# Splitting half of the u weights of a Mamba block into one-pass products

## The chip, the cores and the metric

One Trainium2 chip, one core of it. The metric is the device time of one execution in microseconds, the median of several runs. The kernel computes a whole two-layer perceiver block with x in (2, 64, 1024), so 128 token rows fill the 128 partitions. Engines: TensorE (PE; PEld is its weight load), VectorE (DVE), ScalarE (ACT), GpSimd (POOL), and SyncE (SP), which issues the DMAs.

## The reference, cut to what matters

Six sublayers follow each other, each adding to x. The change lies in the second one, a Mamba block, of which this is the part that matters:

```python
proj = hidden_states @ W_in.T                     # (128, 1024) @ (1024, 4096)
u, gate = jnp.split(proj, 2, axis=-1)             # 2048 columns each
x = conv_general_dilated(u ...)                   # depthwise, 4 taps in time
u = jax.nn.silu(x + conv_b)
ssm_p = u @ Wx.T                                  # 96 columns: dt, B, C
...                                               # softplus, scan over 64 steps of 16 states
y = (ys + u * D_param) * jax.nn.silu(gate)
return y @ W_out.T
```

All data is float32.

## The kernel before

Every engine has its own instruction stream, written out by hand, with semaphores between them. Weights come as units of 1 MB: 128 partitions x (4 k tiles x 512 columns), into a ring of seven slots; SyncE issues them in the order of `unit_list`, each when the last use of its slot is over (`last_use`, `uses`, L533). w_in has 16 units. A group j of 512 output columns takes two of them: k tiles 0 to 3 from unit 2j, 4 to 7 from unit 2j+1. Groups 0 to 3 (NG = 4) are u, groups 4 to 7 the gate. The small tables of the Mamba block (`mamba_in`, L520 to L524) are queued ahead of unit w_in 4.

The left side is h, the normalized x, transposed to `hT` (k tiles 0 to 3 copied by ScalarE at L686, 4 to 7 by VectorE at L1478). `w_in_product(j, k)` (L1003, matmul at L1012) multiplies in full float32 into a PSUM bank; the profile records each such matmul as two. After the last k tile it raises `proj_psum`.

What follows for a u group, engine by engine:

- ScalarE `proj_copy(j)` (L693) copies the group out of PSUM. TensorE transposes it, `turn(j)` (L931), two k tiles into the next group. 
- VectorE `conv_in(j)` (L1484) copies the transpose to `uT`. ScalarE `last_tap(j)` (L736) multiplies the newest tap, VectorE `conv(j)` (L1501) adds three taps; for the last group VectorE does the newest tap too (L1495).
- ScalarE `half_tanh(j)` (L701), then VectorE `silu(j)` (L1516).

Their orders are: ScalarE: proj_copy(j), last_tap(j), half_tanh(j-1) for j = 0 to 2, then proj_copy(3), half_tanh(2), half_tanh(3). VectorE: conv_in(0), conv(0), conv_in(1), silu(0), conv(1), conv_in(2), silu(1), conv(2), conv_in(3), silu(2), conv(3), silu(3). TensorE: the four u groups with turns 0 to 2 in them, one gate product, turn(3), five gate products, `small_projection` 0 to 2 (L1029), one gate product, `small_projection(3)`, and then the time steps and the scan. `small_projection(3)` needs silu(3); everything behind it hangs on it.

From w_out on the kernel already uses split products: ScalarE `high(m)` (L795) copies a unit, rounded to float32r, VectorE `low(m)` (L1621) subtracts that from the unit, and TensorE multiplies high by high, high by low (both at L965) and low by high (L972), one pass each, from `unit_halves`. The left side is split in the same way into `split` (L683, L1474). The memory `rounded` (the same as `plain`) is not in use while w_in is multiplied.

Of the kernel before, what the change touches and what calls it, by code (L numbers as in the profile page):

```python
# [12 lines left out]
ALU = mybir.AluOpType  # L13
ACT = mybir.ActivationFunctionType
AX = mybir.AxisListType.X
F32 = mybir.dt.float32
# [8 lines left out]
KT = D // P  # L25
UK = 4
UN = 512
UNIT = UK * UN
# [13 lines left out]
NG = DT // GD  # L42
# [46 lines left out]
def perceiver(nc, dram, out):  # L89
    units = unit_list()  # L90
    first = {}
# [5 lines left out]
    with ExitStack() as stack:  # L97
# [3 lines left out]
        def sem(name):  # L101
            return stack.enter_context(nc.semaphore(name))
# [4 lines left out]
        hT = sb("hT", [P, KT, P])  # L107
# [10 lines left out]
        split = sb("split", [P, 2, KT, P], F32R)  # L118
        psum = stack.enter_context(nc.psum_tensor("psum", [P, 8, 512], F32))

        def carve(tile, start, *dims):
            size = 1
            for d in dims:
                size *= d
            ap = tile[:, start:start + size]
            if len(dims) == 2:
                ap = ap.rearrange("p (a b) -> p a b", a=dims[0])
            if len(dims) == 3:
                ap = ap.rearrange("p (a b c) -> p a b c", a=dims[0], b=dims[1])
            return ap  # L130
# [78 lines left out]
            rounded[:, 2 * UNIT:4 * UNIT], rounded[:, 0:2 * UNIT], arena_r[:, 11392:11392 + 2 * UNIT])]  # L209


        w_ar = carve(arena, 0, KT, NE * RANK + NE)
        lora_b = carve(arena, 1088, D)
        bk = carve(arena, 19040, D)
# [66 lines left out]
        hT_hi = sem("hT_hi")  # L281
# [15 lines left out]
        q1T_ready = sem("q1T_ready")  # L297
        q_done = sem("q_done")

        edge_zero = sem("edge_zero")  # L300
        conv_halved = sem("conv_halved")
        first_tap = sem("first_tap")
        proj_psum = sem("proj_psum")
# [113 lines left out]
        def uses(*signals, split=False):  # L417
            nonlocal middle
            for signal in signals:
                if signal is None:  # L420
                    middle += 1
                    signal = (unit_used, middle)
                if split:
                    split_units.append(len(last_use))
                    split_done.append(signal)
                    signal = (unit_low, len(split_done))
                last_use.append(signal)

        for j in range(NB):
            uses(None, (proj_psum, j + 1))  # L430
        uses(None, None)
        uses(None, None)
        for nh in range(2):
# [36 lines left out]
        def slot(n):  # L470
            return place(n).rearrange("p (k n) -> p k n", k=UK)

        def arrived(eng, n):
            if n in spare:

                eng.wait_ge(unit_in[SLOTS + 1], 16 * SPARE)
            else:
                eng.wait_ge(unit_in[slot_of[n]], 16 * slot_of[:n + 1].count(slot_of[n]))
# [5 lines left out]
        def proj_bank(j):  # L484

            return j % 3 if j <= NG else 4

        def turn_bank(j):

            return 3 + j % 2 if j < NG else 5  # L490
# [158 lines left out]
        def _(act):  # L649
# [34 lines left out]

            act.wait_ge(hT_psum, 1)
            act.activation(hT[:, 0:4, :], psum[:, 6, :], ACT.Copy).then_inc(hT_lo, 1)  # L686

            def proj_copy(j):

                act.wait_ge(proj_psum, j + 1)  # L690
                if j >= 3:
                    act.wait_ge(projT_psum, j - 2)
                act.activation(proj[:, j % 3, :], psum[:, proj_bank(j), :], ACT.Copy).then_inc(proj_sb, 1)  # L693
# [38 lines left out]
            def last_tap(g):  # L732

                act.wait_ge(projT_read, g + 1)
                for k in range(GD * g, GD * g + GD):
                    last = act.activation(uc[:, k, :].rearrange("p (b t) -> p b t", b=B), uT[:, k, :, CK - 1:], ACT.Identity,  # L736
                                          bias=conv_b[:, k:k + 1], scale=conv_w[:, k, CK - 1:CK])
                last.then_inc(first_tap, 1)

            for j in range(3):  # L740
                proj_copy(j)
                last_tap(j)
                if j:
                    half_tanh(j - 1)
# [136 lines left out]
            for r in range(GQ):  # L881
                last = act.activation(krep[:, :, r, :], krot.rearrange("p (g d) -> p g d", g=HKV), ACT.Copy)
# [43 lines left out]
        def _(pe):  # L926
# [13 lines left out]
            for nh in range(2):  # L940
                for kh in range(2):
                    for b in range(B):
# [3 lines left out]
                        for k in range(UK):  # L946
# [6 lines left out]
                            last = pe.matmul(psum[rows, 2 + nh, :], ones64, right, **at)  # L953
# [47 lines left out]
            w_in = first["w_in"]  # L1001

            def w_in_product(j, k):  # L1003

                u = 2 * j + k // UK
                if k == 0 and j >= 3:
                    pe.wait_ge(*((proj_sb, j - 2) if j <= NG else (proj_sb, j) if j > NG + 1 else (projT_read, NG)))
                if k % UK == 0:
                    pe.wait_ge(hT_lo, 1)
                    pe.wait_ge(hT_hi, 1)  # L1010
                    arrived(pe, w_in + u)
                last = pe.matmul(psum[:, proj_bank(j), :], hT[:, k, :], slot(w_in + u)[:, k % UK, :], start=(k == 0),  # L1012
                                 stop=(k == KT - 1))
                if k % UK == UK - 1:
                    last.then_inc(proj_psum if k == KT - 1 else unit_used, 1)
# [3 lines left out]
            def gate_products(count):  # L1019

                for _ in range(count):
                    w_in_product(*next(gate_tiles))
# [48 lines left out]
            def scan_input(s):  # L1071
# [17 lines left out]
                                     stop=True)  # L1089
                last.then_inc(dbu_ready, 1)  # L1090

            for j in range(NG):
                for k in range(KT):
                    if j and k == 2:
                        turn(j - 1)
                    w_in_product(j, k)
            gate_products(1)
            turn(3)
            gate_products(5)
# [89 lines left out]
            for k in range(KT):  # L1189
                last = pe.matmul(psum[:, 2, 0:NE * RANK + NE], hT[:, k, :], w_ar[:, k, :], start=(k == 0), stop=(k == KT - 1))  # L1190
# [148 lines left out]
            for nh in range(2):  # L1339
                for part, signal in enumerate((hs_high, hs_low)):  # L1340
                    for k in range(KT):
                        if nh == 0 and k % 4 == 0:
                            pe.wait_ge(signal, 9 + k // 4)
                        last = pe.matmul(psum[:, 4 + nh, :], split[:, part, k, :], onehot[:, k, UN * nh:UN * nh + UN],  # L1344
                                         start=(part == 0 and k == 0), stop=(part == 1 and k == KT - 1))
# [8 lines left out]
            for a in range(MH // 2):  # L1354
                pe.wait_ge(g_hi if a >= 4 else g_lo, 1)
                for m in range(2):
                    for r in range(2):
                        rows = slice(MD * r, MD * r + MD)
                        at = 256 * (a % 2) + P * m
                        last = pe.matmul(psum[:, 4 * r + a // 2, at:at + P], up[rows, a, P * m:P * m + P], gT[rows, a, :],  # L1360
                                         start=True, stop=True)
# [22 lines left out]
        def _(dve):  # L1384
# [91 lines left out]

            dve.wait_ge(hT_psum, 2)
            dve.tensor_copy(hT[:, 4:8, :], psum[:, 7, :]).then_inc(hT_hi, 1)  # L1478
            dve.wait_ge(mamba_in, 80)
            dve.wait_ge(edge_zero, 2)  # L1480

            def conv_in(g):
                dve.wait_ge(projT_psum, g + 1)
                dve.tensor_copy(uT[:, GD * g:GD * g + GD, :, CK - 1:],  # L1484
                                psum[:, turn_bank(g), :].rearrange("p (k b t) -> p k b t", k=GD, b=B)).then_inc(projT_read, 1)

            def conv(g):


                dve.wait_ge(projT_read, g + 1)  # L1490
                if g < NG - 1:
                    dve.wait_ge(first_tap, g + 1)
                else:
                    for k in range(GD * g, GD * g + GD):
                        last = dve.tensor_scalar(uc[:, k, :].rearrange("p (b t) -> p b t", b=B), uT[:, k, :, CK - 1:],  # L1495
                                                 conv_w[:, k, CK - 1:CK], conv_b[:, k:k + 1], ALU.mult, ALU.add)
                    step(last)
                for j in range(CK - 1):
                    for k in range(GD * g, GD * g + GD):
                        to = uc[:, k, :].rearrange("p (b t) -> p b t", b=B)  # L1500
                        last = dve.scalar_tensor_tensor(out=to, in0=uT[:, k, :, j:j + L], scalar=conv_w[:, k, j:j + 1], in1=to,  # L1501
                                                        op0=ALU.mult, op1=ALU.add)
                    if j < CK - 2:
                        step(last)
                last.then_inc(conv_half, 1)

            def silu(n):

                dve.wait_ge(tanh_ready, n + 1)
                if n < NG:  # L1510
                    to = uc[:, GD * n:GD * n + GD, :].rearrange("p k t -> p (k t)")
                    of = to
                else:
                    to = sg[:, GD * (n - NG):GD * (n - NG) + GD, :].rearrange("p k t -> p (k t)")
                    of = psum[:, turn_bank(n), :]
                dve.scalar_tensor_tensor(out=to, in0=tanh[:, n % 2, :], scalar=1.0, in1=of, op0=ALU.add,  # L1516
                                         op1=ALU.mult).then_inc(gated, 1)
# [2 lines left out]
            dve.tensor_scalar(small[:, 320:416], small[:, 320:416], 0.5, None, ALU.mult).then_inc(conv_halved, 1)  # L1520
            dve.wait_ge(conv_halved, 1)
            conv_in(0)
            conv(0)
            conv_in(1)
            silu(0)
            conv(1)
            conv_in(2)
            silu(1)
# [373 lines left out]
```

## Time and profile before

| what | value |
|---|---|
| median of 3 runs | 400.17 us (397.13 to 401.21) |
| profiled execution | 399.9 us, its span 398.1 us |
| mean granted TensorE clock | 0.949 |
| TensorE busy (PE) | 351.0 us, 88% of the span |
| VectorE, ScalarE, GpSimd busy | 269.5, 198.3, 115.4 us |
| DMA, whole span | 81.33 MB, mean 204 GB/s |
| L1012 (w_in products), 128 records | 63.6 us |

The profile is of one execution. Busy time says how long an engine worked, not whether anybody waited for it. The chain that ended last is followed back from the last instruction, at each step to what released it. In a timeline the brackets give the idle time ahead of an instruction and what ended it. PEclk is the granted TensorE clock as a share of full speed: 1.00 is 2.4 GHz, 0.50 is 1.2 GHz. Matmuls are pipelined, so the duration of a single record overlaps the next; distances between starts say what one costs.

### The profile page before, as it was taken

Reading aid. Unit: us, or ns where it says so; the run is one execution under the profiler, and the core shown is the slowest. Engines: PE = TensorE matmul, PEld = TensorE weight load, DVE = VectorE, ACT = ScalarE, POOL = GpSimd, SP = SyncE. Lnnn points to the kernel's source line nnn. Section 1 sums busy time; section 2 is a strip of 40 time slices with the busy share of each in tenths; the row PEclk is TensorE's granted clock in tenths of the full one; section 3 lists DMA queues with packets and bytes.
Section 4 is the critical chain, followed back from the end, with each engine's and each line's share of the span. In section 5 each row is a group of like instructions: output and inputs, shape, how many; then the busy total and the mean of one; then the engine's idle time right before and its main releaser. Section 6 shows DMA issues by size and latency. Waiting matters only on the chain.

```text
span 398.1 us, 4954 instructions
## 1 busy us (share of the span) xinstructions
PE 351.0 (88%) x1894; PEld 222.8 (56%) x1894; DVE 269.5 (68%) x334; ACT 198.3 (50%) x397; POOL 115.4 (29%) x97
## 2 busy tenths in 40 slices
PE   0784999999999989999899897899979698697996
PEld 0432444553556656556566585787323476585885
DVE  2756046947887999998971887685721798765282
ACT  2970034169999687677621554363021476430160
POOL 3500000023999888889900000002000000400000
PEclk9997799999999999999999989699999899669899
DMA  6999987744003020253138798298999991000001
GB/s 260 421 423 376 391 342 266 272 133 185 2 0 107 2 81 26 105 198 126 53 115 331 268 421 340 68 358 327 413 423 370 428 420 62 2 2 0 2 2 53
DMA packets 12824, 81.33 MB, mean 204 GB/s; under 512 B 2094, under 2 KB 2350, under 8 KB 3519
## 3 DMA queue, kind: packets, MB, share of 16 engines
q1 hardware_dynamic: 11614, 78.23, 50.6%
q10 hardware_dynamic: 1154, 2.70, 2.0%
q8 instruction: 15, 0.25, 0.2%
q14 instruction: 9, 0.07, 0.1%
q0 software_dynamic: 32, 0.07, 0.0%
HBM read 80.34 MB, written 0.52 MB: 203 GB/s over the span
## 4 chain that ended last, share of the span: by engine, by line
PE 57%; DVE 15%; POOL 10%; issue 7%; DMA 6%; ACT 3%; POOLq 0%; SPq 0%; DVEq 0%; ACTq 0%
PE psum L1012 10%; PE psum L965 9%; PE psum L1132 6%; PE psum L1235 6%; DMA ring<-in_ctx 6%; PE psum L1088 5%; POOL arena L618 5%; PE psum L931 4%; PE psum L972 4%; PE psum L1156 3%; PE psum L1344 2%; DVE arena L1578 2%; POOL arena L621 2%; PE psum L1379 2%; POOL plain L618 2%
## 5 line engine op out<-in xcount | busy, mean ns | idle before, releaser
L768 ACT ACTIVATE arena<-arena 128x126 f32<-128x126 f32 x256 | 76.5, 389 | 9.7 <-DVE arena L1578 9.3
L1012 PE MATMUL psum<-ring,hT 128*128 128x512 f32 x128 | 63.6, 627 | 0.8 <-issue 0.8
L1578 DVE TENSOR_TENSOR_SCAN arena<-arena,psum 128x1024 f32<-128x1024 f32 x24 | 54.2, 2272 | 3.2 <-PE psum L1088 3.0
L618 POOL TENSOR_TENSOR arena<-arena 128x1024 f32<-128x1024 f32 x20 | 47.2, 2360 | 5.4 <-DVE arena L1578 5.4
L1621 DVE TENSOR_TENSOR rounded<-ring,rounded 128x2048 fp32r<-128x2048 f32 x16 | 36.5, 2285 | 10.4 <-ACT rounded L795 10.4
L1132 PEld LDWEIGHTS psum<-arena,ident 128*128 128x128 f32 x292 | 35.6, 192 | 13.8 <-issue 10.0
L795 ACT ACTIVATE rounded<-ring 128x2048 fp32r<-128x2048 f32 x16 | 30.6, 1912 | 21.9 <-PE psum L972 14.0
L558 POOL TENSOR_TENSOR small<-small 128x1 f32<-128x1 f32 x6 | 3.3, 554 | 127.0 <-DVE small L1402 127.0
L1012 PEld LDWEIGHTS psum<-ring,hT 128*128 128x128 f32 x128 | 23.3, 199 | 29.1 <-issue 29.1
L1132 PE MATMUL psum<-arena,ident 128*128 128x128 f32 x292 | 37.3, 278 | 1.6 <-POOL arena L621 1.6
L1088 PE MATMUL psum<-plain 64*128 64x512 f32 x128 | 36.1, 641 | 1.7 <-DVE arena L1578 1.4
L931 PE MATMUL psum<-ident,h 128*128 128x128 f32 x48 | 10.9, 402 | 27.6 <-DVE h L1405 16.0
L965 PE MATMUL psum<-rounded,split 128*128 128x512 f32 x96 | 27.7, 436 | 0.3 <-DVE rounded L1621 0.3
L931 PE MATMUL psum<-ident,arena 128*128 128x128 f32 x120 | 21.2, 306 | 7.3 <-ACT arena L901 2.6
L931 PEld LDWEIGHTS psum<-ident,h 128*128 128x128 f32 x48 | 8.5, 204 | 31.1 <-DVE h L1405 19.4
L931 PEld LDWEIGHTS psum<-ident,arena 128*128 128x128 f32 x120 | 14.9, 153 | 19.0 <-issue 6.9
L1235 PE MATMUL psum<-ring,arena 128*64 128x512 f32 x96 | 24.4, 593 | 0.0
L965 PEld LDWEIGHTS psum<-rounded,split 128*128 128x128 f32 x96 | 20.1, 215 | 5.6 <-ACT split L683 0.6
L683 ACT ACTIVATE split<-psum 128x512 fp32r<-128x512 f32 x10 | 6.0, 598 | 31.2 <-PE psum L931 31.1
L621 POOL TENSOR_TENSOR arena<-arena 128x256 f32<-128x256 f32 x23 | 21.0, 917 | 1.6
L1578 DVE TENSOR_TENSOR_SCAN plain<-arena,psum 128x1024 f32<-128x1024 f32 x8 | 18.2, 2272 | 4.1 <-PE psum L1088 4.1
L675 ACT ACTIVATE arena<-ring,small 128x2048 uint8<-128x2048 f32 (+1 forms) x9 | 16.9, 1900 | 8.0 <-DMA ring<-in_ctx 8.0
(207 smaller groups left out, 579.4 us busy)
## 6 DMA issues: line engine op xcount, KB each, us to landing
ring<-in_w_in SPq DMA_DIRECT2D x16, 1024.0 KB, 7.5
ring<-in_ctx SPq DMA_DIRECT2D x13, 1024.0 KB, 10.0
ring<-in_w_out SPq DMA_DIRECT2D x8, 1024.0 KB, 4.8
ring<-in_ctx_t SPq DMA_DIRECT2D x7, 1024.0 KB, 5.1
ring<-in_w_base SPq DMA_DIRECT2D x4, 1024.0 KB, 4.8
ring<-in_x_wk SPq DMA_DIRECT2D x4, 1024.0 KB, 7.7
ring<-in_a_wo SPq DMA_DIRECT2D x4, 1024.0 KB, 9.4
ring<-in_x_wq SPq DMA_DIRECT2D x3, 1024.0 KB, 8.9
```

Of the source, the lines that this page charges most:

```text
L618: pool.tensor_tensor(state[s % STATES], state[s % STATES], c, ALU.mult).then_inc(prod_ready, 1)
L621: pool.tensor_tensor(v[:, :, L * 4:L * 6], v[:, :, L * 4:L * 6], v[:, :, L * 6:L * 8], ALU.add).then_inc(pairs_ready, 1)
L768: last = act.activation(to, of, ACT.Exp, scale=a_par[:, k, state_no:state_no + 1])
L795: act.activation(unit_halves[m % 3][:, 0, :, :], slot(split_units[m]), ACT.Copy).then_inc(unit_high, 1)
L931: last = pe.transpose(psum[:, bank, P * k:P * k + P], tile[:, c:c + P], ident[:, :])
L965: pe.matmul(psum[:, bank, :], left(0, k0 + k), unit[:, w, k, :], start=(start and k == 0 and w == 0), stop=False)
L1012: last = pe.matmul(psum[:, proj_bank(j), :], hT[:, k, :], slot(w_in + u)[:, k % UK, :], start=(k == 0), stop=(k == KT - 1))
L1088: last = pe.matmul(psum[:, input_bank(s, b), :], du[rows_of(b), left], bdiag[rows_of(b), right, :], start=True, stop=True)
L1132: last = pe.matmul(psum[:, 6 + g % 2, cols], ident[:, :], v[:, n, :, :], start=(s % 2 == 0 and n == 0), stop=(s % 2 == 1 and n == count - 1))
L1235: last = pe.matmul(psum[L * b:L * b + L, bank, :], left[:, UK * kh + k, L * b:L * b + L], slot(u0 + b)[:, k, :], start=(kh == 0 and k == 0 ...
L1578: dve.tensor_tensor_scan(state[s % STATES], dA[:, s % 3, :], psum[:, p:p + 2, :].rearrange("p a b -> p (a b)"), 0.0, ALU.mult, ALU.add).th ...
L1621: dve.tensor_tensor(unit[:, 1, :, :], slot(split_units[m]), unit[:, 0, :, :].bitcast(F32), ALU.subtract).then_inc(unit_low, 1)
```

## The change

For the four u groups, the second unit (k tiles 4 to 7) no longer goes through `w_in_product` but through split products. ScalarE gets one copy of the upper half of hT into `split`, and four copies u_high(j) of a weight unit, j = 0 and 1 ahead of proj_copy(0), 2 and 3 between proj_copy(j-2) and last_tap(j-2). VectorE gets the matching subtractions: u_low(0) and u_low(1) ahead of conv_in(0), u_low(2) between conv_in(0) and conv(0), u_low(3) between silu(0) and conv(1). The halves alternate between two buffers in `rounded`. A split unit's ring slot comes free at its u_low. TensorE issues 12 one-pass products in place of four full ones.

```diff
+        u_halves = [rounded[:, 2 * UNIT * n:2 * UNIT * n + 2 * UNIT].rearrange("p (a k n) -> p a k n", a=2, k=UK)
+                    for n in range(2)]
...
         for j in range(NB):
-            uses(None, (proj_psum, j + 1))
+            uses(None, (u_unit_low, j + 1) if j < NG else (proj_psum, j + 1))
...
             act.activation(hT[:, 0:4, :], psum[:, 6, :], ACT.Copy).then_inc(hT_lo, 1)
+            act.wait_ge(hT_hi, 1)
+            act.activation(split[:, 0, 4:8, :], hT[:, 4:8, :], ACT.Copy).then_inc(u_left_high, 1)
+
+            def u_high(j):
+
+                n = first["w_in"] + 2 * j + 1
+                arrived(act, n)
+                if j >= 2:
+                    act.wait_ge(proj_psum, j - 1)
+                act.activation(u_halves[j % 2][:, 0, :, :], slot(n), ACT.Copy).then_inc(u_unit_high, 1)
+
+            u_high(0)
+            u_high(1)
...
             for j in range(3):
                 proj_copy(j)
+                if j < 2:
+                    u_high(2 + j)
                 last_tap(j)
...
+            def u_split_products(j):
+
+                pe.wait_ge(u_left_low, 1)
+                pe.wait_ge(u_unit_low, j + 1)
+                unit = u_halves[j % 2]
+                for k in range(UK):
+                    for w in range(2):
+                        pe.matmul(psum[:, proj_bank(j), :], split[:, 0, UK + k, :], unit[:, w, k, :], start=False, stop=False)
+                for k in range(UK):
+                    last = pe.matmul(psum[:, proj_bank(j), :], split[:, 1, UK + k, :], unit[:, 0, k, :], start=False,
+                                     stop=(k == UK - 1))
+                last.then_inc(proj_psum, 1)
+
             for j in range(NG):
-                for k in range(KT):
+                for k in range(UK):
                     if j and k == 2:
                         turn(j - 1)
                     w_in_product(j, k)
+                u_split_products(j)
...
             dve.tensor_copy(hT[:, 4:8, :], psum[:, 7, :]).then_inc(hT_hi, 1)
+            dve.wait_ge(u_left_high, 1)
+            dve.tensor_tensor(split[:, 1, 4:8, :], hT[:, 4:8, :], split[:, 0, 4:8, :].bitcast(F32),
+                              ALU.subtract).then_inc(u_left_low, 1)
+
+            def u_low(j):
+
+                dve.wait_ge(u_unit_high, j + 1)
+                unit = u_halves[j % 2]
+                dve.tensor_tensor(unit[:, 1, :, :], slot(first["w_in"] + 2 * j + 1), unit[:, 0, :, :].bitcast(F32),
+                                  ALU.subtract).then_inc(u_unit_low, 1)
+
+            u_low(0)
+            u_low(1)
...
             conv_in(0)
+            u_low(2)
             conv(0)
             conv_in(1)
             silu(0)
+            u_low(3)
             conv(1)
```

## Rows read from the trace of the kernel before

**Rows 1.** The chain that ended last, 43 to 83 us: start, duration, what.

```profile
50.72 6.87 PE psum L1012 x16
...
65.37 0.70 DVE arena L1484
...
79.77 1.13 PE psum L1029 x8
```

**Rows 2.** Timeline of VectorE, 36 to 75 us: start, duration, work, idle time before.

```profile
37.76 0.69 DVE L1478 COPY hT<-psum 128x512 f32<-128x512 f32 x1 [1.60 <-PE psum L931]
...
50.83 0.69 DVE L1484 COPY arena<-psum 128x512 f32<-128x512 f32 x1 [8.71 <-PE psum L931]
53.30 3.49 DVE L1501 SCALAR_TENSOR_TENSOR arena<-arena,small 128x128 f32<-128x128 f32 x12 [1.79 <-ACT arena L736]
58.06 0.69 DVE L1484 COPY arena<-psum 128x512 f32<-128x512 f32 x1 [1.27 <-PE psum L931]
60.99 0.69 DVE L1516 SCALAR_TENSOR_TENSOR arena<-arena 128x512 f32<-128x512 f32 x1 [2.23 <-ACT arena L701]
61.60 3.48 DVE L1501 SCALAR_TENSOR_TENSOR arena<-arena,small 128x128 f32<-128x128 f32 x12
65.37 0.69 DVE L1484 COPY arena<-psum 128x512 f32<-128x512 f32 x1 [0.28 <-PE psum L931]
...
72.30 0.68 DVE L1484 COPY arena<-psum 128x512 f32<-128x512 f32 x1
```

**Rows 3.** Timeline of ScalarE, 36 to 60 us, same columns.

```profile
48.60 0.60 ACT L693 ACTIVATE arena<-psum 128x512 f32<-128x512 f32 x1 [11.10 <-PE psum L1012]
51.55 1.65 ACT L736 ACTIVATE arena<-arena,small 128x128 f32<-128x128 f32 x4 [2.35 <-DVE arena L1484]
55.91 0.60 ACT L693 ACTIVATE arena<-psum 128x512 f32<-128x512 f32 x1 [2.71 <-PE psum L1012]
```

**Rows 4.** The chain, 200 to 262 us: f32 products followed by one-pass products.

```profile
203.99 10.30 PE psum L1156 x24
214.29 1.86 PE psum L965 x8
216.15 0.92 PE psum L972 x4
```

**Rows 5.** Source lines of the split in later stages: duration ns min/median/max, starts.

```profile
L795 ACT ACTIVATE rounded<-ring x16: 1897/1913/1923, 192.1 to 357.2; 128x2048 fp32r<-128x2048 f32 x16
...
L1621 DVE TENSOR_TENSOR rounded<-ring,rounded x16: 2275/2283/2293, 199.3 to 359.2; 128x2048 fp32r<-128x2048 f32 x16
```

**Rows 6.** Busy times by window: span, PE, PEld, DVE, ACT, POOL, PEclk, DMA, GB/s.

```profile
44.00:45.00 1.00, 1.00 (x4) 0.36 (x3) 0.00 (x0) 0.00 (x0) 0.00 (x0) 0.79 1.02 418
```

**Rows 7.** The page: GB/s moved in each of 40 slices of the span.

```profile
GB/s 260 421 423 376 391 342 266 272 133 185 2 0 107 2 81 26 105 198 126 53 115 331 268 421 340 68 358 327 413 423 370 428 420 62 2 2 0 2 2 53
```

**Rows 8.** Timeline of TensorE: small projections, and two bursts that follow idle time.

```profile
75.96 2.81 PE L1029 MATMUL psum<-arena 128*128 128x96 f32 x24
...
250.08 1.97 PE L931 MATMUL psum<-ident,h 128*128 128x128 f32 x8 [3.15 <-DVE h L1405]
...
294.58 1.33 PE L931 MATMUL psum<-ident,arena 128*128 128x128 f32 x8 [2.31 <-ACT arena L867]
```

**Rows 9.** The chain behind the idle stretch that ends at 250.08 us.

```profile
252.05 3.61 PE psum L965 x8
255.66 1.15 PE psum L972 x4
256.81 1.83 PE psum L965 x8
258.65 0.91 PE psum L972 x4
```

**Rows 10.** Busy times by window after the same two idle stretches.

```profile
250.00:252.00 2.00, 1.92 (x9) 1.69 (x9) 0.62 (x3) 0.60 (x1) 0.00 (x0) 0.50 0.00 0
294.00:295.00 1.00, 0.42 (x4) 0.42 (x4) 0.00 (x0) 1.00 (x4) 0.00 (x0) 1.00 0.99 418
```

More of the change, by code:

```diff
@@ L298, in perceiver @@
         q_done = sem("q_done")
+        u_left_high = sem("u_left_high")
+        u_left_low = sem("u_left_low")
+        u_unit_high = sem("u_unit_high")
+        u_unit_low = sem("u_unit_low")
         edge_zero = sem("edge_zero")
```

## The prediction, made before the kernel ran

> **What bounds the kernel now.** I read the page first, where TensorE has by far the most busy time, which does not yet say that it ends the waits. The change touches only the stage that projects w_in and convolves (about 36 to 80 us), so next I read the chain of work that ended last in that stage, then the timelines of VectorE and ScalarE in it, and last, from later stages, the price of the same operations where the kernel already uses them.
>
> In the chain the reader is to see a change of hands. Up to 65.3 us it runs on TensorE alone: 16 records of 0.43 us (6.87 us) and then the transposes of `turn`, and it delivers a group of columns each 7.31 us (copies at 48.60 and 55.91) [rows 1, 3]. From 65.37 us it runs on VectorE and ScalarE (copy, last tap, half tanh, silu, taps) until 79.7 us, and TensorE takes over with `small_projection(3)` at 79.77 us [rows 1]. The VectorE timeline shows how close that was even before [rows 2]. A loop of conv_in, last_tap (ScalarE, 1.65 us), tanh, silu and three taps takes 58.06 to 65.08 us (61.60 + 3.48) = 7.02 us, against the 7.31 us in which TensorE delivers; VectorE was ready 0.28 us before the third group [rows 2, 3]. The third loop, where nothing is waited for from TensorE, takes 65.37 to 72.30 = 6.93 us [rows 2]. So a faster TensorE is worth little here, and added VectorE time is worth its full price wherever it lands in this loop outside an existing wait.
>
> **The change part by part.** *TensorE.* In each of four u groups the last four k tiles leave as full-precision products (8 records of 0.429 = 3.43 us by 6.87/16) and come back as 12 one-pass products. Later stages price these: 24 f32 records take 10.30 us (0.429 each), and directly behind them 8 one-pass products take 1.86 and 4 take 0.92, thus 2.78 us for 12, with no gap at the switch [rows 4]. A later dozen takes 1.83 + 0.91 = 2.74 [rows 9]. I take 2.73. Saved: 3.43 - 2.73 = 0.70 us a group, 2.8 us in four. The Trainium skill (FP8 and Floating Point Precision, TensorE Precision Notes) counts a true FP32 product as four passes; by that count three passes of four would save a quarter of 3.43, or 0.86 us a group. The trace's one-pass product (1.86/8 = 0.23 us) is slightly dearer than half an f32 record (0.21), and the sum goes by the trace.
>
> *First split, ahead of group 0.* hT's upper half is there at 37.76 + 0.69 = 38.45 us [rows 2]. ScalarE then rounds it (0.60, as its other copies of 128x512 [rows 3]), then u_high(0) and u_high(1), 1.91 us each [rows 5]: done at 39.1, 41.0 and 43.0. VectorE: left low 0.69 (as its copy), u_low(0) from 41.0 to 43.3, u_low(1) to 45.6, 2.28 us each [rows 5]. TensorE spends until about 44.8 on the first unit, because the granted clock is at its lower level (1.2 GHz) until about 44.4 and at 2.4 GHz after (0.79 of full speed in the microsecond from 44) [rows 6]. So u_low(0) is 1.5 us early, and all of this lies in idle time: ScalarE sat idle 11.1 us before 48.60, VectorE 8.7 before 50.83 [rows 2, 3]. Cost 0; if the clock rose as soon as 40 us, TensorE would wait some 0.6 us.
>
> *Arrivals.* The bytes queued up to unit w_in 3 are 13.1 MB (x 0.5, eight ctx and four w_in units of 1.05), up to w_in 5 with the 1.6 MB of tables ahead of w_in 4 16.8 MB, up to w_in 7 18.9 MB. By the GB/s row 14.7 MB had moved by 39.8 us and 18.6 by 49.8 (slices of 9.95 us) [rows 7]. So they land near 36, 45 and 51 us, and the ScalarE reads them at 41.0, 48.5 and 55.1: no wait. The slots of the split units come free at u_low instead of at the group's end, but only loads of gate units (first used after 67 us) follow from it: 0.
>
> *ScalarE in the loop.* u_high(2) and u_high(3) stand between proj_copy(j) and last_tap(j). ScalarE sat idle 2.35 us there in group 0, waiting for VectorE's conv_in [rows 3]. With 1.91 us it is free 0.4 us before conv_in ends. Behind it are queued last_tap, half_tanh and the next proj_copy; none is delayed. Cost 0.
>
> *VectorE in the loop.* With T0 (start of the copy out of PSUM) = 48.60 - 0.70 = 47.90, and 7.31 - 0.70 = 6.61 a group, T1 = 54.51, T2 = 61.12, T3 = 67.73. conv_in comes 2.15 to 2.23 us behind T [rows 2, 3].
> Group 0: conv_in 50.13, u_low(2) 50.83 to 53.11 (the old wait for last_tap, 1.79 us, covers most of it), conv(0) to 56.61. conv_in(1) is due at 54.51 + 2.15 = 56.66: hidden by 0.05 us.
> Group 1: u_low(3) stands behind silu(0) and ahead of conv(1), where VectorE never waited: full price. conv_in(2) at 56.66 + 6.93 + 2.28 = 65.87 (was 65.37), although TensorE has the group ready at 63.3.
> Group 2: conv_in(3) at 65.87 + 6.93 = 72.80 (was 72.30). From here every step is as before: silu(3) and small_projection(3) are 0.5 us later.
>
> *What TensorE does with its time.* proj_copy(3) is queued behind last_tap(2) and half_tanh(1) on ScalarE and now starts near 68.8 instead of at T3, so turn(3) waits some 0.9 us until 69.4. Ahead of small_projection(3) TensorE then has ten f32 records (4.3), the first three small projections (2.81) [rows 8] and two f32 records (0.86), so that it stands idle from about 77.9 to 80.3. The 2.8 us gained end there. Behind it comes the same chain, all moved by +0.5 us; no load later is issued by a clock of its own.
>
> **Sum.** -2.8 us of TensorE work, of which 0 reaches the end; the loop gains 1.8 from the earlier start of group 1 (72.30 - (56.66 + 2 x 6.93)) and pays 2.28: +0.5 us. The profiled execution took 399.9 us, so 400.4; the median of the runs is 400.17, 0.3 above it, and against that the forecast is 400.7 us. About 1% (4 us) is what a measurement of this kernel can tell from no change.
>
> **Rivals.**
> *Faster: u_low costs nothing on the path.* If the third split fits into waits (a tap loop shorter than I read, or TensorE still the one that ends the stage), the loop ends at 56.66 + 2 x 6.93 = 70.5, 1.8 us earlier: 398.4; with TensorE in charge to the end all 2.8: 397.4. For it: 2.2 us of VectorE idle in each group [rows 2]. Against: that idle lies ahead of silu, and u_low(3) stands behind it. It decides if u_low(3) runs ahead of silu(0). 12%.
>
> *Slower: the new idle stretches lower TensorE's clock.* Two gaps (0.9 and 2.4 us) appear where TensorE had none. A gap of 2.31 us ahead of 294.58 left the clock at 1.00; behind one of 3.15 us ahead of 250.08 it was 0.50 [rows 8, 10]. There the 8 transposes took 1.97 us against 1.33 at 294.58, the next 8 products 3.61 against 1.86 and 4 more 1.15 against 0.92: +2.6 us [rows 4, 8, 9]. If that falls on the work behind 80 us: 0.5 + 2.6 = +3.1, 403.8. The gap I expect is nearer the harmless one, and mostly small products lie ahead of it: 10%. The Trainium skill (TensorE: Matmul & The Clock Gate, What's actually happening) says that the throttled level is the default and activity lifts it, which speaks against a change that opens gaps; the trace has an outcome of each kind.
>
> *The one-pass products save nothing* (their loads of weights not hidden, or TensorE waiting for u_low(0)): T1 stays 55.91, conv_in(1) 58.06, then 58.06 + 2 x 6.93 + 2.28 = 74.20: +1.9 us, 402.1. Against it are the 12 such products at 0.23 us directly behind f32 ones [rows 4]. 8%.
>
> **How the numbers follow.** Forecast 70% (400.7, own range 399.5 to 402), rivals 12, 10 and 8%. The range for 8 in 10 reaches from the first (398.4) to nearly the second (403.8), widened below for the spread of single runs: 398.2 to 403.6. None but a fallen clock with a second mishap passes +1%, none alone reaches -1%. Faster by over 1%: 4%; within: 88%; slower: 8%.
>
> **What would show it.** In the profile after: L1012-type f32 records fall from 128 to 96 and 48 one-pass products appear in the stage; the copies out of PSUM come 6.6 us apart, then the fourth late; conv_in(1) near 56.7, conv_in(2) near 65.9, conv_in(3) near 72.8, small_projection(3) near 80.3; a TensorE gap of 2 us or more ahead of it with PEclk 1.00. The forecast is wrong if the last two come earlier than 79.8, if the clock is at 0.50 past 70 us, or if the difference comes from beyond 95 us, where I expect only the shift.

## The result, and the profile after

| | kernel before | changed kernel |
|---|---|---|
| median of 20 runs | 399.88 us (396.98 to 401.40) | 401.12 us (400.15 to 402.88) |
| ratio | 1 | 1.0040, 95% interval 1.0021 to 1.0059 |
| profiled execution (its span) | 399.9 us (398.1) | 402.87 us (401.1) |
| granted clock in it, mean | 0.949 | 0.940 |

The change made the kernel slower by 1.6 us (0.8 to 2.4) by the ratio, which goes by all runs; the two medians are 1.2 us apart. Either is within 1% of before. The forecast was +0.5 us, 400.7.

The page of the changed kernel shows what was bought and what was paid. In the fence are its TensorE, VectorE and ScalarE totals and the clock row. TensorE's own busy time did not fall, though 2.8 us of work are gone.

```profile
PE 351.7 (88%) x1910; PEld 227.2 (57%) x1910; DVE 278.8 (70%) x339; ACT 205.8 (51%) x402; POOL 115.4 (29%) x97
...
PEclk9996799989999999999999989899989899569899
```

VectorE and ScalarE have 9.3 and 7.5 us more. In the clock row the slice from 80 us is an 8, where before had a 9.

The next fence is the timeline of VectorE in the changed kernel (start, duration, work, idle time before). It answers to [rows 2].

```profile
50.03 0.69 DVE L1533 COPY arena<-psum 128x512 f32<-128x512 f32 x1 [4.43 <-PE psum L953]
50.64 2.28 DVE L1523 TENSOR_TENSOR rounded<-ring,rounded 128x2048 fp32r<-128x2048 f32 x1
52.84 3.48 DVE L1550 SCALAR_TENSOR_TENSOR arena<-arena,small 128x128 f32<-128x128 f32 x12
56.59 0.69 DVE L1533 COPY arena<-psum 128x512 f32<-128x512 f32 x1 [0.27 <-PE psum L953]
59.52 0.69 DVE L1565 SCALAR_TENSOR_TENSOR arena<-arena 128x512 f32<-128x512 f32 x1 [2.24 <-ACT arena L721]
60.13 2.28 DVE L1523 TENSOR_TENSOR rounded<-ring,rounded 128x2048 fp32r<-128x2048 f32 x1
62.33 3.48 DVE L1550 SCALAR_TENSOR_TENSOR arena<-arena,small 128x128 f32<-128x128 f32 x12
65.73 0.69 DVE L1533 COPY arena<-psum 128x512 f32<-128x512 f32 x1
...
72.66 0.68 DVE L1533 COPY arena<-psum 128x512 f32<-128x512 f32 x1
```

L1533 is conv_in, L1523 u_low, L1550 the taps, L1565 silu. u_low(2) at 50.64 fills a wait. u_low(3) at 60.13 does not: VectorE has just been idle for 2.24 us, waiting for the tanh, and then pays 2.28 us. conv_in(2) and (3) come at 65.73 and 72.66, against 65.37 and 72.30 before.

On TensorE the time saved turns up as idle time, ahead of turn(3) and of small_projection(3):

```profile
67.49 1.02 PE L1034 MATMUL psum<-ring,hT 128*128 128x512 f32 x2
69.15 0.66 PE L953 MATMUL psum<-ident,arena 128*128 128x128 f32 x4 [0.64 <-ACT arena L713]
...
76.59 1.05 PE L1034 MATMUL psum<-ring,hT 128*128 128x512 f32 x2
80.12 1.13 PE L1051 MATMUL psum<-arena 128*128 128x96 f32 x8 [2.48 <-DVE arena L1565]
```

small_projection(3) starts at 80.12, 0.35 us later than before (79.77). So far the forecast holds. But at 81.7 us, 1.6 us behind the end of the idle stretch, the granted clock falls to its lower level, 1.2 GHz, and stays there until 85.1. The fence is the busy times by window of the changed kernel (columns as in [rows 6]; the figure before the last two is PEclk).

```profile
78.00:80.00 2.00, 0.00 (x0) 0.00 (x0) 1.30 (x4) 0.63 (x1) 0.00 (x0) 1.00 0.00 0
80.00:82.00 2.00, 1.88 (x10) 1.38 (x11) 0.71 (x6) 0.00 (x0) 0.00 (x0) 0.93 0.00 0
82.00:84.00 2.00, 2.00 (x4) 0.73 (x3) 0.95 (x10) 0.60 (x1) 0.86 (x1) 0.50 0.35 49
84.00:86.00 2.00, 2.00 (x6) 0.76 (x4) 1.34 (x2) 0.28 (x2) 0.55 (x1) 0.72 0.85 352
86.00:88.00 2.00, 2.00 (x17) 1.83 (x16) 0.00 (x0) 1.82 (x2) 1.35 (x1) 1.00 0.31 127
```

It falls on the three gate products that lead the chain there. These six records took 2.60 us before, now 4.30 (the chain that ended last, changed kernel):

```profile
80.12 1.13 PE psum L1051 x8
81.25 4.30 PE psum L1034 x6
85.55 0.11 PE psum L1070
...
95.43 2.30 DVE plain L1629
```

The first scan step starts at 95.43. From VectorE's copy of the small projection (81.29) that is 14.14 us; before it was 93.60 - 80.94 = 12.66. So 0.35 us came from the loop and 1.48 from the clock: 1.83 us at the start of the scan. The profiled pair ends 3.0 us apart; the other 1.2 us come late, where the clock falls at many places in both kernels. In this pair it also fell at 296.7 us in the changed kernel, and not in before: behind 94 us the clock was low for 34.2 us in all, against 31.4.

### The profile page after: what moved, and what is told of

Read it like the earlier page. It is cut to its first block, busy times and chain, and to the rows that moved or that the text cites. A ratio compares the mean times of both kernels' runs of the same rounds, so it can differ in the third digit from the quotient of the medians.

```text
span 401.1 us, 4998 instructions
## 1 busy us (share of the span) xinstructions
PE 351.7 (88%) x1910; PEld 227.2 (57%) x1910; DVE 278.8 (70%) x339; ACT 205.8 (51%) x402; POOL 115.4 (29%) x97
## 4 chain that ended last, share of the span: by engine, by line
PE 56%; DVE 15%; POOL 10%; issue 7%; DMA 6%; ACT 4%; POOLq 0%; SPq 0%; DVEq 0%; ACTq 0%
PE psum L987 10%; PE psum L1034 7%; PE psum L1271 7%; PE psum L1168 6%; DMA ring<-in_ctx 6%; PE psum L1110 5%; POOL arena L625 5%; PE psum L994 4%; PE psum L953 4%; PE psum L1192 3%; DVE arena L1550 3%; PE psum L1380 2%; DVE arena L1629 2%; POOL arena L628 2%; PE psum L1415 2%
## 5 line engine op out<-in xcount | busy, mean ns | idle before, releaser
L1034 PE MATMUL psum<-ring,hT 128*128 128x512 f32 x96 | 52.0, 657 | 0.8 <-issue 0.8
L953 PE MATMUL psum<-ident,h 128*128 128x128 f32 x48 | 9.4, 360 | 27.7 <-DVE h L1441 16.0
L987 PE MATMUL psum<-rounded,split 128*128 128x512 f32 x96 | 28.9, 452 | 0.8 <-ACT split L690 0.5
L1034 PEld LDWEIGHTS psum<-ring,hT 128*128 128x128 f32 x96 | 17.6, 206 | 20.9 <-issue 20.6
L953 PEld LDWEIGHTS psum<-ident,h 128*128 128x128 f32 x48 | 7.2, 182 | 31.2 <-DVE h L1441 19.4
```

The source lines that it names most:

```text
L953: last = pe.transpose(psum[:, bank, P * k:P * k + P], tile[:, c:c + P], ident[:, :])
L987: pe.matmul(psum[:, bank, :], left(0, k0 + k), unit[:, w, k, :], start=(start and k == 0 and w == 0), stop=False)
```

## The experiments

The theories were these. **L**: the loss is u_low(3), at its full price in the loop of VectorE and ScalarE (the steps from one conv_in to the next). **C**: the idle stretch that the change opens on TensorE makes the clock fall, and the work behind it pays. **T**, named for the first run: later stages lose, whatever the u stage does. The ratio is to before on the same chip and goes by all runs, so it need not be that of the two medians. Four numbers are read from every trace: the start of small_projection(3), the idle stretch ahead of it, the clock behind it, and the way from VectorE's copy of the small projection to the first scan step.

| kernel | median, us | ratio (95%) | idle stretch | clock behind it | way to the scan |
|---|---|---|---|---|---|
| before | 399.88 | 1 | 0.1 | 1.00 | 12.66 |
| changed | 401.12 | 1.0040 (1.0021 to 1.0059) | 2.48 | 0.50 | 14.14 |
| f1_low_first | 398.13 | 0.9940 (0.9917 to 0.9962) | 1.11 | 1.00 | 12.66 |
| f2_pad_gap | 401.23 | 1.0020 (1.0000 to 1.0041) | 0.77 | 1.00 | 12.65 |
| f3_before_delay | 401.27 | 1.0020 (1.0004 to 1.0037) | 1.94 | 1.00 | 12.66 |
| f4_three_groups | 398.52 | 0.9942 (0.9922 to 0.9963) | 0.41 | 1.00 | 12.66 |
| g1_after_again | 402.37 | 1.0069 (1.0041 to 1.0097) | 2.49 | 0.50 | 13.94 |
| g2_pad_again | 401.96 | 1.0043 (1.0011 to 1.0075) | 0.77 | 1.00 | 12.65 |
| g3_low_first_and_tile | 397.47 | 0.9951 (0.9924 to 0.9979) | 0.25 | 1.00 | 11.79 |
| g4_longer_gap | 404.63 | 1.0118 (1.0088 to 1.0148) | 3.90 | 0.50 | 14.56 |

The median of before was 400.32 us beside the f kernels and 399.69 beside the g kernels.

### f1_low_first: the third subtraction ahead of silu

```diff
             conv_in(1)
-            silu(0)
             u_low(3)
+            silu(0)
             conv(1)
```

> The changed kernel with one swap on VectorE: u_low(3) runs ahead of silu(0) instead of behind it. Theory L (the loss is u_low(3) at full price in the loop of VectorE and ScalarE): VectorE sat idle 2.24 us ahead of silu(0), u_low(3) lasts 2.28, so the loop gets back 2.2 us; conv_in(3) near 70.5 us, small_projection(3) near 77.9, TensorE arrives there at 77.6 without a gap, the clock stays at 1.00 behind it, and the median is 1.5 to 2 us below the kernel before (398 to 398.5). Theory C (the loss is the clock that falls behind the gap, in some executions): also gone here, since the gap goes. Theory T (later stages lose, whatever the u stage does): the median stays 1 to 1.5 us above before although small_projection(3) is early.

Measured: 398.13 us, 0.6% below before. The VectorE timeline of this kernel shows u_low(3) in the old wait, which is gone:

```profile
55.80 0.69 DVE L1533 COPY arena<-psum 128x512 f32<-128x512 f32 x1 [0.27 <-PE psum L953]
56.41 2.28 DVE L1523 TENSOR_TENSOR rounded<-ring,rounded 128x2048 fp32r<-128x2048 f32 x1
58.73 0.69 DVE L1565 SCALAR_TENSOR_TENSOR arena<-arena 128x512 f32<-128x512 f32 x1
59.34 3.48 DVE L1550 SCALAR_TENSOR_TENSOR arena<-arena,small 128x128 f32<-128x128 f32 x12
62.74 0.68 DVE L1533 COPY arena<-psum 128x512 f32<-128x512 f32 x1
```

From conv_in(1) to conv_in(2) are 6.94 us, against 9.14 in the changed kernel: 2.20 back. small_projection(3) starts at 77.14. In this execution the first copy out of PSUM was also 0.79 us earlier than in the changed kernel (47.02 against 47.81), since the clock rose earlier at the start. From that copy it is 30.12 us to small_projection(3), against 32.31 in the changed kernel and 31.17 before. An idle stretch of 1.11 us is left, where I had expected none. Theory L holds. T is out: the gain arrives at the end. C is not tested by this, as the stretch shrank too.

### f4_three_groups: only groups 0, 1 and 2 split

```diff
-                if j < 2:
+                if j < 1:
                     u_high(2 + j)
...
-                for k in range(UK):
+                for k in range(UK if j < NG - 1 else KT):
                     if j and k == 2:
                         turn(j - 1)
                     w_in_product(j, k)
-                u_split_products(j)
+                if j < NG - 1:
+                    u_split_products(j)
...
             silu(0)
-            u_low(3)
             conv(1)
```

> The changed kernel with only u groups 0, 1 and 2 split; group 3 is multiplied in full float32 as before, and u_high(3) and u_low(3) are left out. Theory L: the loop is free of u_low(3), so conv_in(3) comes near 70.5 us and the path is 1.8 to 1.9 us shorter than before; TensorE, one saving of 0.66 us short, reaches small_projection(3) near 78.2, a little behind silu(3) at 77.9: net 1.5 us faster than before. If TensorE's saving were worth nothing because of other limits, the median equals before.

Measured: 398.52 us, 0.58% below before, with the path 30.11 us long from the first copy to small_projection(3) (46.81 to 76.92), as short as in f1. So, with u_low(3) where the change has it, the split of group 3 bought nothing, as its TensorE time was spare, and cost everything that was lost on the loop.

### f3_before_delay: the price of the place alone

```diff
             silu(0)
+            idle_a = x[:, :].rearrange("p (u n) -> p u n", u=1).to_broadcast([P, 2, D])
+            idle_b = h[:, :].rearrange("p (u n) -> p u n", u=1).to_broadcast([P, 2, D])
+            dve.tensor_tensor(plain[:, 0:2 * D].rearrange("p (u n) -> p u n", u=2), idle_a, idle_b, ALU.subtract)
             conv(1)
```

> The kernel before, with nothing split, and one VectorE subtraction of 128x2048 (x minus h into unused memory, 2.28 us) between silu(0) and conv(1), where the change puts u_low(3). Theory L: conv_in(2) and conv_in(3) come 2.0 us later (2.28 less the 0.28 that VectorE had to spare), small_projection(3) at 81.8, a TensorE gap of 2.1 us ahead of it, and the median 2.0 us above before, more by a share of executions in which the clock falls (theory C, up to +0.7 on the median). If VectorE's time there were not on the path: no change.

The trace is as expected: 32.99 us from the first copy (47.58) to small_projection(3) (80.57), against 31.17 before, so +1.82. The subtraction took 2.29 us. The idle stretch was 1.94 us, and the clock stayed at 1.00. The median moved by only 0.95 us, half of what I expected. That miss is of use: it led me to group the runs by their granted clock, below, where the difference is 1.6 us. The runs of this kernel happened to have the higher clock, 0.951 in the mean against 0.947 of before beside it.

### f2_pad_gap, g1_after_again and g2_pad_again: the idle stretch filled with nothing

```diff
             gate_products(1)
+            for _ in range(2):
+                pe.matmul(psum[:, 7, :], hT[:, 0, :], hT[:, 0:4, :], start=True, stop=True)
             small_projection(3)
```

> The changed kernel with two more f32 matmuls (four records, 1.7 us) of hT by hT into a PSUM bank that nobody reads, in the idle stretch of TensorE ahead of small_projection(3); 0.8 us of idleness remain. Nothing else moves: small_projection(3) stays at 80.1. Theory L alone: same median as the changed kernel (401.1), all of it from the loop. Theory C: the clock stays at 1.00 between 81 and 85 us in every execution, the slower group of runs near 402.7 is gone, and the median falls to the level of the loop's own +0.35 us over before, near 400.3.

> The changed kernel as it is, beside the padded one on the same chip. Grouped by the mean granted clock of each execution (0.953, 0.949, 0.944, 0.940), theory L expects the path's +0.35 to +0.45 us over before in every group. Theory C adds that some executions have one more fall of the clock, the one at 81 us, which shows as a lower mean clock than before has and as a group near 402.7.

> The padded kernel again (two f32 matmuls in the idle stretch ahead of small_projection(3)), now beside the changed kernel on one chip. Theory C: 0.3 to 0.7 us below the changed kernel in the median. Theory L alone: equal within 0.3 us.

The padded kernel does more work in the same places, and the clock holds (f2_pad_gap, TensorE's timeline at the end of the stretch):

```profile
80.16 1.13 PE L1051 MATMUL psum<-arena 128*128 128x96 f32 x8 [0.77 <-DVE arena L1567]
```

and the windows of the same execution:

```profile
80.00:82.00 2.00, 1.84 (x10) 1.38 (x11) 0.71 (x6) 0.00 (x0) 0.00 (x0) 1.00 0.00 0
82.00:84.00 2.00, 1.98 (x6) 0.66 (x5) 0.95 (x10) 0.60 (x1) 0.86 (x1) 1.00 0.46 74
```

small_projection(3) starts within 0.04 us of where it did, and the way to the scan is 12.65 us instead of 14.14. In the trace this is plain. In the run times it is small: beside each other on one chip, the changed kernel had a median of 402.37 us and the padded one of 401.96. The forecast of C was 0.3 to 0.7 us, and it was 0.41 (0.8 by the means), but the spread is too wide for that to show much (the changed kernel's runs reach from 400.33 to 403.10, and the intervals of the two ratios overlap). The level of 400.3 that I expected for f2_pad_gap was missed by 0.9 us. Its median, 401.23, is where L alone had put it (401.1), and the slower group that was to go was still there, 6 of 12 runs at 402.25. So these times do not show at the end of the kernel the 1.5 us that the trace shows at the scan.

### The runs grouped by their granted clock

Every execution has a mean granted clock, and these come in steps, as the clock falls once more or once less somewhere in the kernel. The means in us, with the number of runs:

| kernel | 0.961 | 0.953 | 0.949 | 0.944 | 0.940 |
|---|---|---|---|---|---|
| before, beside f | | 399.39 (8) | 399.98 (3) | 400.81 (7) | 401.53 (5) |
| f1_low_first | | 397.56 (3) | | 399.09 (3) | |
| f4_three_groups | | 397.59 (2) | | 398.86 (4) | |
| f3_before_delay | | 401.01 (8) | 401.71 (1) | 402.31 (3) | |
| f2_pad_gap | | 400.06 (2) | 400.32 (4) | | 402.25 (6) |
| before, beside g | 397.02 (7) | 398.94 (6) | 399.80 (4) | 400.53 (8) | 401.21 (2) |
| changed, first set | | 400.27 (2) | 400.94 (11) | 400.82 (1) | 402.68 (6) |
| g1_after_again | | | 401.03 (4) | | 402.65 (6) |
| g2_pad_again | 398.03 (2) | | 400.48 (2) | 401.20 (1) | 402.26 (7) |

(The three runs of f3_before_delay under 0.944 stood at 0.945.) One step down from 0.953 costs before some 0.6 to 0.9 us, so most of the spread of this kernel is the number of such falls. Within a column the path shows as it should: f1 and f4 lie 1.7 to 2.0 us below before, f3 1.5 to 1.7 above. The changed kernel lies 1.2 to 1.4 us above before on one chip (L alone expected 0.35 to 0.45 in every group), the padded one 0.3 to 1.05. Between changed and padded are 0.4 to 0.55 us at equal clock. That fits a fall at 81 us that costs more than one elsewhere. In 30 runs of the changed kernel none was above 0.953; before had 7 of 27 there on one chip but none of 23 on the other, so this shows little. (g3 and g4 stood at other values: 0.957, 0.948 and 0.940, and 0.945, 0.941 and 0.937.)

The 13 profiles show the same from inside. Behind 94 us the time depends on how long the clock was low there, whatever the kernel. From the first scan step to the end it is 303.9 us with 28.0 us of low clock (f2), 304.5 to 305.1 with about 31 (before, f1 twice, f3, f4, g1), 305.5 to 305.9 with about 34 (changed, h1, h3, g3, g4) and 306.7 with 37.6 (g2).

### h1, h2 and h3: three more looks

> A further profile of the changed kernel, to count how often the clock falls behind the 2.5 us idle stretch ahead of small_projection(3) (so far in 2 of 2 profiles, at 81.7 and 80.4 us). Theory C: in most profiles it falls, and the way from the copy of the small projection to the copies of the C matrix takes 9.6 to 9.9 us instead of 8.36. Chance: half or fewer.

> A second profile of the kernel with u_low(3) ahead of silu(0), whose idle stretch is 1.1 us. Theory C: no fall of the clock between 70 and 90 us, and 8.36 us from the copy of the small projection to the copies of the C matrix.

> A further profile of the padded kernel (0.8 us of idleness left there; so far 0 of 2 profiles show the fall). Theory C: again none, 8.36 us from the copy of the small projection to the copies of the C matrix.

Changed kernel: the stretch was 2.48 us, the clock at 0.50 from 81.0 us, and the way from the copy to the scan 14.14 us. f1 once more: 1.10 us, clock 1.00, 12.66. Padded: 0.77, 1.00, 12.66. (The expectations give the way to the copies of the C matrix: 9.85, 8.37 and 8.37 us. The single times were 402.33, 397.75 and 400.64 us, with one of before at 397.01.) So the fall behind the 2.5 us stretch stands in 3 of 3 profiles of the changed kernel, and in none of the 3 padded ones, none of the 2 of f1, and not behind the 1.94 us of f3.

### g4_longer_gap: the stretch made longer

```diff
             conv(3)
+            dve.tensor_tensor(sg.rearrange("p k t -> p (k t)").rearrange("p (u n) -> p u n", u=2), idle_a, idle_b, ALU.subtract)
             silu(3)
```

> The changed kernel with one more VectorE subtraction of 128x2048 (2.28 us, into memory not in use yet) between conv(3) and silu(3). 0.69 us of it lies in VectorE's wait for the tanh, so small_projection(3) comes 1.6 us later and TensorE's idle stretch grows from 2.5 to 4.1 us. Theory L alone: 1.6 us slower than the changed kernel. Theory C: the clock falls behind the stretch in nearly every execution, and the difference is 2.5 to 3 us.

Measured: 404.63 us, 2.3 us above the changed kernel on the same chip. The clock falls at 80.1 us, while TensorE still idles, so small_projection(3) has the lower level from its first record, and it stays until 86.9 us (windows of this kernel):

```profile
80.00:82.00 2.00, 1.26 (x6) 1.26 (x7) 0.68 (x2) 0.00 (x0) 0.00 (x0) 0.52 0.00 0
82.00:84.00 2.00, 2.00 (x6) 1.28 (x6) 1.07 (x10) 0.00 (x0) 0.00 (x0) 0.50 0.00 0
84.00:86.00 2.00, 2.00 (x3) 0.67 (x2) 0.99 (x6) 0.60 (x1) 0.86 (x1) 0.50 0.24 45
86.00:88.00 2.00, 2.00 (x6) 0.78 (x4) 0.87 (x1) 0.34 (x2) 1.05 (x1) 0.77 0.82 344
```

small_projection(3) came 1.42 us later (80.74 against 79.32), and its eight records took 2.02 us instead of 1.13. The copy of the projection to the scan took 14.56 us. Start to start of the scan is 2.75 us behind g1 (97.36 against 94.61). L alone gave 1.6, C 2.5 to 3: the trace (2.75) sides with C, the medians (2.3) lie between. The clock had fallen in the changed kernel too, for 3.4 us; here it stayed low for 6.8, and small_projection(3) itself ran slow.

### g3_low_first_and_tile: a version faster than both

```diff
             for g in range(3):
                 small_projection(g)
-            gate_products(1)
+            gate_products(2)
             small_projection(3)
...
             time_steps(1)
-            gate_products(2)
+            gate_products(1)
             spread_c(0)
```

on top of f1_low_first.

> u_low(3) ahead of silu(0), and one gate tile (0.86 us) moved from between time_steps(1) and spread_c(0), where the chain runs on TensorE, into the 1.1 us that TensorE still idles ahead of small_projection(3). Theory L: the chain behind 80 us gets 0.8 us shorter: 2.5 us below before, 0.8 below the kernel with u_low(3) first alone. If the chain there is really held by ScalarE's and VectorE's softplus steps: no change against that kernel.

Measured: 397.47 us, 0.49% below before (0.2 to 0.8). The chain that ended last shows two records instead of four between the time steps and the spread of C, and the scan starts 11.79 us behind the copy, not 12.66:

```profile
81.80 1.79 PE psum L1063 x16
83.58 0.86 PE psum L1034 x2
84.44 1.92 PE psum L1078 x8
...
89.84 2.30 DVE plain L1629
```

This is what TensorE's spare time could be used for. The forecast was 2.5 us below before; by the ratio it was 2.0. Whether it beats f1 was not measured on one chip: by ratio f1 is as far below before. The trace shows 0.87 us less on the path, and the seven runs at 0.948 (397.37 us) lie 2.4 below before's at 0.949.

## Why the prediction was right, and where it was not

**TensorE's term was right.** The copies out of PSUM come 6.62 us apart (47.81 and 54.43), forecast 6.61: 0.69 us saved a group.

**The first split was free**, as argued: VectorE had both u_low(0) and u_low(1) done at 45.5 us, and TensorE went from its eighth f32 record into the first one-pass product without a wait (38.59 + 6.43 and 44.46). No unit came late.

**The loop was right, to 0.15 us.** conv_in(2) was forecast at 65.87 and came at 65.73; conv_in(3) at 72.80 and 72.66; small_projection(3) at 80.3 and 80.12. f1, f3 and f4 show it from three sides: u_low(3) moved into the wait (2.20 us back), the same work put into the kernel before (+1.82), and the group left unsplit (the same gain as f1).

**The fate of the 2.8 us was right in size and wrong in harm.** By its own signs the forecast was wrong here: it named a clock at 0.50 past 70 us as one, and the clock was at 0.50 from 81.7 to 85.1. The idle stretches came to 0.64 and 2.48 us, forecast 0.9 and 2.4. The step that failed is "The gap I expect is nearer the harmless one, and mostly small products lie ahead of it: 10%". I compared only lengths, 2.31 us that did no harm against 3.15 that did, each from one execution. In three of three profiles 2.48 us was enough. And the harmless row was the exception: the same stretch of 2.31 us stands in all 13 profiles, and in 11 of them the clock fell behind it. The fence has it in f3_before_delay, which splits nothing: TensorE's timeline, and then the window behind it.

```profile
294.40 1.78 PE L931 MATMUL psum<-ident,arena 128*128 128x128 f32 x8 [2.31 <-ACT arena L867]
...
296.00:298.00 2.00, 2.00 (x7) 0.65 (x8) 0.92 (x3) 0.00 (x0) 0.00 (x0) 0.50 0.97 406
```

Only before and f2_pad_gap kept 1.00 there. The Trainium skill (TensorE: Matmul & The Clock Gate, What's actually happening) has the throttled level as the default that activity lifts, and the traces agree: past the first rise of the clock each fall in this stage came with the idle stretch or up to 1.6 us behind it, and two matmuls whose result nobody reads kept it away in 3 of 3 profiles. The price was also smaller than I had put it, 1.3 to 1.5 us (12.66 against 13.94 and 14.14) rather than 2.6: in the profiled execution the six f32 records of the gate products took 1.70 us more, of which 1.48 reached the scan. The rival's sum has a slip besides: 403.8 adds 3.1 us to the forecast, 400.7, which has the loop's 0.5 in it already; 400.17 + 3.1 is 403.3.

So the sum in the place of the forecast is +0.35 to 0.45 from the loop and +1.3 to 1.5 from the clock: 1.6 to 1.9 us, against 1.6 measured (0.8 to 2.4), and 2.8 (1.6 to 3.9) by the second set of runs. It holds at the start of the scan; at the end of the kernel it is not shown, as the next paragraph says, and the agreement there can be chance. That the median, 401.12, lies even in the forecast's own range (399.5 to 402) was luck: the rival that it held to be 10% likely came true at about half its price, and the median of before was 399.88, not 400.17.

**What stays open.** The padded kernel has the loop's loss and not the clock's, so by this sum it should be 0.45 us above before. By the ratios it was 0.8 (0 to 1.6) and 1.7 us (0.4 to 3.0) above. At equal clock it was 0.3 to 1.05 above, 0.7 in the mean of the seven groups; the 0.2 or 0.3 us left are within what a few runs a group can scatter. The rest is clock: a fall of 3.4 us lowers an execution's mean clock by 0.0043 (an estimate, 3.4 / 2 / 399), and the padded kernel's runs are only 0.0017 above the changed kernel's beside them (0.9453 and 0.9436). So it had, in the mean, more falls elsewhere. Whether the padding or the change moves such falls, or chance did in 12 and 10 runs, is not shown. Nor is it settled what besides the length of a stretch decides: at one place 2.48 us lowered the clock in 3 of 3 profiles and 1.94 us did not in one, but a stretch of 1.24 us near 229 us came with a fall in 13 of 13.

## What to carry to other kernels

Work taken off an engine is a gain only at the places where that engine ends the wait; look for the row of the timeline where another engine has less than the saving to spare, here 0.28 us. Work added to a busy engine belongs ahead of its wait, not behind it: one swapped line was worth 2.2 us of the loop. And time saved on TensorE that turns up as an idle stretch can lower its clock, which here made a loss of 0.35 us one of 1.8 at the start of the scan. Work that waits further down, as the gate tile, can go into such a stretch. Here that was tried only on a stretch of 1.1 us that did no harm, where it shortened the path by 0.87 us.

## What the runs showed of the hardware that I had not expected

An idle stretch of 2.48 us on TensorE was followed by the lower clock, for 3.4 us, in 3 of 3 profiles; stretches of 0.77, 1.11 and 1.94 us at the same place never were (6 profiles). At other places one of 1.24 us came with a fall in 13 of 13 profiles, and one of 2.31 us in 11 of 13, so the length of one stretch alone does not tell. The mean granted clock of an execution takes a few values (0.961, 0.953, 0.949, 0.944, 0.940), each step worth 0.6 to 0.9 us, and 1.9 between the first two, which lie twice as far apart. Most of the spread of this kernel's times comes from that, and comparing runs within one value shows differences of 1 us that medians of ten runs blur: f3_before_delay was 0.95 us slower by medians and 1.6 by groups, with 1.82 on the path.
